# Cross attention in units of four heads by 512 queries, keys resident, softmax sums by matmuls of their own

## Chip, cores and metric

One core of one Trainium2 chip runs the whole program. The metric is device microseconds of one execution; lower is better. The median of three runs of the kernel before is 3451.21 us (3448.59 to 3453.72).

## What is computed

A pre-norm decoder layer in float32: self attention, cross attention with a context of 154 positions, and a gated feed-forward with selected experts. B = 2, S = 2048, D = 512, 16 heads of 32. The change touches cross attention and its two neighbours. In terms of the reference:

```python
q = heads(xq)                     # (2, 16, 2048, 32)
k, v = heads(ctx @ Wk), heads(ctx @ Wv)   # (2, 16, 154, 32)
scores = q @ k.T / sqrt(32)       # padding mask; causal mask key <= query
attn = softmax(scores) @ v        # joined, then Wo, residual, layer norm, feed-forward
```

The causal mask hides something only from the first 154 queries of a batch, so only in the first block of 512. The padding mask is all false in the inputs but is applied.

## The kernel before

The program is a row of stages, each a `nc.Block` that ends with a barrier of all engines: `project_qkv`, `self_attention`, `attention_to_queries`, `cross_context`, `cross_attention`, `shared_feed_forward`, `selected_experts`. They pass tensors on through DRAM.

`cross_context` (L1076) makes keys and values of the context and the masks. It stores the keys as three parts of 32 rows (`xk_parts`: high, high, low), the values with columns of ones between those of each pair of heads (`xv_ones`), and masks for causal and for other blocks.

`cross_attention` (L1194) works in 64 units of two heads by 512 queries. For each unit `load` (L1260) brings the queries' parts, the pair's keys, and its values with ones. The maxima come first: `scores` (L1312) makes queries x keys on TensorE, four tiles of 128 queries for each head, each with a mask matmul behind it (L1327). `maxima` (L1380) takes the negative maximum over 154 keys of four tiles at once on VectorE (L1383) and splits it into three bfloat16 parts with five small operations (L1392 to L1397). `turn_max` (L1330) transposes the parts with eight matmuls, and `max_rows` (L1399) copies them into three more rows of the query tile, so that the transposed scores come out with the maximum taken off. `transposed_scores` (L1338) makes keys x queries, in two halves of 77 keys. ScalarE takes the exponential (L1429), and `weighted_values` (L1349) multiplies with the 64 columns of values and ones of a head: one half of the output's partitions per head, and the sums of the softmax come out beside the weighted values. ScalarE copies both out (L1433), and SP stores values and sums. TensorE's order is written out by hand:

```python
for w in range(UPB):                       # L1367
    pe.wait_ge(max_rows_done, at(i, w, 1, 1))
    transposed_scores(i, b, causal, w, 0)
    turn_max(*after(i, w, 1))
    scores(*after(i, w, 2), (0,))
    transposed_scores(i, b, causal, w, 1)
    scores(*after(i, w, 2), (1,))
    weighted_values(i, w)
```

During the first units GpSimd also splits the next stage's weights into a high and a low part (`Ahead`, L52; `split`, L65), after some memsets at the stage's head (L1299).

`shared_feed_forward` (L1438) works on eight blocks of 512 rows. It first loads all sums, inverts them on VectorE (L1643), stores them, and reads the inverses back for each block with every row repeated 32 times (`load_sums`, L1540). GpSimd multiplies the weighted values with them and adds the output bias to the residual (`scale`, L1599: L1602 once, L1604 four times); then ScalarE (`split`, L1759) and VectorE split the product for TensorE's three-part matmuls. In a block's end, `transposes` (L1813) wait for VectorE's `norm` (L1678, the instruction is L1686), between the matmuls of `down` (L1846) and those of `up` (L1822).

`self_attention` (L324) is not changed, but has already the form that cross attention gets: units of four heads, values in four groups of 32 columns (L583), sums by a matmul with ones (L591, L598), reciprocals in PSUM (L677) and a product (L684).

## Time and profile before

| | us |
|---|---|
| median of three runs | 3451.21 |
| the profiled execution, its own time | 3448.84 |
| its span, first to last instruction | 3446.9 |
| TensorE busy (matmuls) | 3077.2 |
| VectorE busy | 2216.5 |
| ScalarE busy | 1609.8 |
| GpSimd busy | 1745.6 |

The mean granted TensorE clock is 0.943 of full speed. Busy times are over the whole span, so they mix stages with different limits: a stage is to be read in its own stretch. PE is TensorE's matmuls, PEld its weight loads, DVE VectorE, ACT ScalarE, POOL GpSimd, SP the engine that issues DMAs.
### The profile page before, as it was taken

The page shows a single profiled execution, that of the slowest core. Times are in us where ns is not written, and L with a number is a line of the kernel's source. Part 1 is how long each engine was busy: PE and PEld are TensorE (multiplying, and loading weights), DVE is VectorE, ACT ScalarE, POOL GpSimd, SP SyncE. Part 2 cuts the span into 40 slices and gives each one's busy share as a digit, 9 for nine tenths or more (in the row PEclk, how much of TensorE's full clock was granted, in tenths as well). Part 3 has the DMA queues.
Part 4 walks back from the last instruction along what each step waited for, and adds up shares of the span by engine and source line. Part 5 has one row for each costly group of instructions (what it writes and reads, how often), then busy time and mean ns, then how long its engine had stood idle before and what let it go on. Part 6 is the DMA issues. An engine that isn't in the chain of part 4 may idle for free. (4 is left out here: it accounts for less than half of the span.)

```text
span 3446.9 us, 44367 instructions
## 1 busy us (share of the span) xinstructions
PE 3077.2 (89%) x15510; PEld 1769.8 (51%) x15510; DVE 2216.5 (64%) x4046; ACT 1609.8 (47%) x2933; POOL 1745.6 (51%) x701
## 2 busy tenths in 40 slices
PE   7997999999999999999999994896499994888578
PEld 6875444444444544444444441784255553666433
DVE  4334788888888888888888871563366663666322
ACT  2221466666666666666666664231145451222111
POOL 0001378787887878888788886000200002444255
PEclk9998799999999999999999997997699997999679
DMA  4546445646346464464645344696544444432631
GB/s 173 182 170 176 108 100 110 132 92 151 85 107 147 89 150 95 101 141 101 150 86 110 75 92 121 179 243 163 137 123 123 123 123 138 147 146 110 216 86 34
DMA packets 195323, 442.85 MB, mean 128 GB/s; under 512 B 32618, under 2 KB 60202, under 8 KB 175532
## 3 DMA queue, kind: packets, MB, share of 16 engines
q1 hardware_dynamic: 171014, 295.73, 29.3%
q0 software_dynamic: 24128, 144.75, 19.9%
q8 instruction: 109, 1.79, 0.2%
q14 instruction: 72, 0.59, 0.1%
HBM read 187.47 MB, written 126.04 MB: 91 GB/s over the span
## 5 line engine op out<-in xcount | busy, mean ns | idle before, releaser
L652 DVE TENSOR_REDUCE part_max<-ps_s 128x1 f32<-128x512 f32 x2048 | 1270.1, 679 | 309.9 <-PE ps_s L553 309.9
L749 ACT ACTIVATE probs<-ps_st 128x512 f32<-128x512 f32 x2048 | 1086.4, 600 | 546.0 <-PE ps_st L572 531.6
L511 POOL TENSOR_TENSOR added<-added,probs 128x2048 f32<-128x2048 f32 x256 | 1182.5, 4619 | 91.1 <-ACT probs L749 64.7
L553 PE MATMUL ps_s<-k_stack,q_stack 96*128 96x512 f32 x2048 | 841.9, 427 | 28.3 <-POOL max_parts L501 20.6
L572 PE MATMUL ps_st<-q_stack,k_stack 98*128 98x512 f32 x2048 | 857.2, 424 | 6.6 <-ACT probs L749 5.4
L572 PEld LDWEIGHTS ps_st<-q_stack,k_stack 98*128 98x128 f32 x2048 | 386.6, 189 | 504.6 <-ACT probs L749 363.1
L583 PE MATMUL ps_pv<-probs,v_sb 128*32 128x512 f32 x4096 | 546.5, 606 | 0.0
L553 PEld LDWEIGHTS ps_s<-k_stack,q_stack 96*128 96x128 f32 x2048 | 395.5, 193 | 214.5 <-DVE part_max L652 143.7
L519 POOL DMA_DIRECT2D probs<-probs x128 | 112.8, 881 | 230.8 <-PE ps_pv L583 218.2
L1626 POOL MEMSET e_bias_rows<- 128x1024 f32 x1 | 1.0, 953 | 370.0 <-POOLq L46 370.0
L511 POOL TENSOR_TENSOR added<-probs 128x2048 f32<-128x2048 f32 x32 | 146.3, 4571 | 48.7 <-ACT probs L749 48.7
L677 DVE RECIPROCAL ps_d<-ps_d 128x128 f32<-128x128 f32 x128 | 120.9, 949 | 63.2 <-PE ps_d L598 63.2
L1325 PE MATMUL xps_s<-xk_stack,xq_stack 96*128 96x154 f32 x528 | 130.4, 335 | 31.8 <-DMA xv_ones_sb<-xv_ones 31.8
L583 PEld LDWEIGHTS ps_pv<-probs,v_sb 128*32 128x32 f32 x4096 | 80.7, 108 | 152.1 <-ACT probs L749 123.4
L1401 DVE CAST xq_stack<-xps_s 3x1024 fp32r<-3x1024 f32 x65 | 79.9, 1230 | 97.4 <-PE xps_s L1334 97.4
L1325 PEld LDWEIGHTS xps_s<-xk_stack,xq_stack 96*128 96x128 f32 x528 | 108.5, 208 | 60.8 <-issue 33.8
L1355 PE MATMUL xps_pv<-xprobs,xv_ones_sb 128*64 128x512 f32 x512 | 124.8, 607 | 10.1 <-ACT xprobs L1429 9.3
L1429 ACT ACTIVATE xprobs<-xps_st,xpad_bias 77x512 f32<-77x512 f32 x192 | 120.5, 678 | 28.3 <-PE xps_st L1343 28.2
L1383 DVE TENSOR_REDUCE xneg_max<-xps_s 128x4 f32<-128x616 f32 x132 | 105.6, 800 | 34.9 <-PE xps_s L1327 33.0
L227 DVE TENSOR_TENSOR qk_l_out<-ps_g,qk_h_out 128x512 fp32r<-128x512 f32 x64 | 43.3, 689 | 126.1 <-ACT qk_h_out L264 126.1
L185 POOL TENSOR_TENSOR rstd<-var_eps,minus_half 128x4 f32<-128x4 f32 x8 | 8.1, 1015 | 224.5 <-DVE var_eps L205 224.5
L1327 PE MATMUL xps_s<-mq_sb,xident_bf 128*128 128x154 bf16 (+1 forms) x528 | 115.7, 249 | 0.0
(269 smaller groups left out, 3684.6 us busy)
## 6 DMA issues: line engine op xcount, KB each, us to landing
probs<-probs POOLq DMA_DIRECT2D x128, 1024.0 KB, 7.1
xq_stack<-q_parts SPq DMA_DIRECT2D x66, 384.0 KB
q_stack<-q_hi SPq DMA_DIRECT2D x64, 256.0 KB
k_stack<-k_hi SPq DMA_DIRECT2D x64, 256.0 KB, 10.7
q_parts<-q_h_out SPq DMA_DIRECT2D x64, 256.0 KB, 4.9
x_in<-in_x_rows SPq DMA_DIRECT2D x8, 1024.0 KB
q_hi<-qk_h_out SPq DMA_DIRECT2D x8, 1024.0 KB
q_lo<-qk_l_out SPq DMA_DIRECT2D x8, 1024.0 KB, 6.4
```

Of the source, the lines that this page charges most:

```text
L511: pool.tensor_tensor(added[:, w % 2], left, probs[:, k % RING], ALU.add).then_inc(added_up, 1)
L519: pool.dma_start(probs[:, k % RING].rearrange("p j q -> p (j q)"), probs[:, (k - 1) % RING].rearrange("p j q -> p (j q)"), accum_op=ALU.ad ...
L553: pe.matmul(ps_s[:, place % BANKS], q_stack[0:ROWS, w % 4, j, t * P:(t + 1) * P], k_stack[0:ROWS, w // BPB, j, n * BLK:(n + 1) * BLK], sta ...
L572: pe.matmul(ps_st[:, n % BANKS], k_stack[:, w // BPB, j, k * P:(k + 1) * P], q_stack[:, w % 4, j], start=True, stop=True).then_inc(item_do ...
L583: mm = pe.matmul(ps_pv[j * HD:(j + 1) * HD], v_sb[:, w // BPB, k, j * HD:(j + 1) * HD], probs[:, k % RING, j], start=(k == 0), stop=(k == ...
L652: dve.tensor_reduce(part_max[:, s:s + 1], ps_s[:, (w * SLOTS + s) % BANKS], AX.X, ALU.max)\
L677: dve.reciprocal(ps_d[:, cols], ps_d[:, cols]).then_inc(inverted, 1)
L749: act.activation(probs[:, k % RING, j], ps_st[:, n % BANKS], ACT.Exp, scale=SCALE).then_inc(item_used, 1)
L1325: pe.matmul(out, q_stack[0:ROWS, w % BUFS, j, t * P:(t + 1) * P], k_stack[0:ROWS, w % BUFS, j], start=True, stop=False)
L1327: mm = pe.matmul(out, ident_bf[:], mask_of(mq, i)[:, t], start=False, stop=True)
L1355: mm = pe.matmul(ps_pv[j * 2 * HD:(j + 1) * 2 * HD, w % 2], v_ones[:, w % BUFS, h, j * HD:(j + 2) * HD], probs[:, (w % 2) * 2 + j, h], sta ...
L1429: act.activation(probs[0:KH, (w % 2) * 2 + j, h], ps_st[0:KH, h], ACT.Exp, scale=SCALE, **bias)\
```

## The change

Cross attention goes over 32 units of four heads by 512 queries. The keys of a batch are loaded once into two tiles that stay: one for the scores, with a further row for the padding bias, one for the transposed scores. Queries are loaded by unit, the values once. Mask matmuls are left for causal blocks only. The maxima are taken over two query tiles at a time into three PSUM banks, split into two parts instead of three, turned by four matmuls, and copied by ScalarE. `weighted_values` has four groups of 32 columns, and `totals`, behind it, multiplies the exponentials of both key halves with ones. VectorE inverts the sums in PSUM in four pieces and multiplies; the output is stored normalized. The loops are unrolled. GpSimd's split of the weights keeps its operations in another order. The feed-forward loses the sums: their load, inversion, store, broadcast loads and the multiply. `cross_context` stores plain values, masks for causal blocks alone, and two small tensors with the padding bias.

The core of the diff, indentation cut by part; the lines removed from `cross_attention` are those of the kernel printed above.

```diff
-def split(self, pool):
-    pool.wait_ge(self.loaded, 16 * len(self.weights))
-    for _, raw, high, _ in self.weights:
+def split_step(self, pool, step):
+    n = step // 2
+    _, raw, high, low = self.weights[n]
+    if step % 2 == 0:
+        pool.wait_ge(self.loaded, 16 * len(self.weights))
         pool.tensor_copy(high, raw).then_inc(self.high_done, 1)
-    for n, (_, raw, high, low) in enumerate(self.weights):
+    else:
         pool.wait_ge(self.high_done, n + 1)
         pool.tensor_tensor(low, raw, high.bitcast(F32), ALU.subtract).then_inc(self.low_done, 1)
-    pool.wait_ge(self.low_done, len(self.weights))
...
-    sp.wait_ge(ones_set, 1)
-    for b in range(B):
-        sp.dma_start(xv_ones[b], xv[:, b].rearrange("k h r c -> k (h r c)")).then_inc(stored, 16)
-    sp.wait_ge(masks_done, 4 * B)
-    sp.dma_start(mask_q, mq[:].rearrange("p b f t k -> p (b f t k)")).then_inc(stored, 16)
-    sp.dma_start(mask_k, mk[:].rearrange("p b f h k -> p (b f h k)")).then_inc(stored, 16)
-    sp.wait_ge(stored, 16 * (3 * (P // HD) + B + 2))
-@block.gpsimd
-def _(pool):
-    pool.memset(xv[:, :, :, :, HD:2 * HD], 1.0).then_inc(ones_set, 1)
+    sp.dma_start(xv_rows, xv[:]).then_inc(stored, 16)
+    sp.wait_ge(masks_done, 3 * B + 1)
+    sp.dma_start(bias_rows.unsqueeze(0), bias_row[0:1]).then_inc(stored, 16)
+    sp.dma_start(bias_scaled, scaled_col[:]).then_inc(stored, 16)
+    sp.dma_start(mask_q, mq[:].rearrange("p b t k -> p (b t k)")).then_inc(stored, 16)
+    sp.dma_start(mask_k, mk[:].rearrange("p b h k -> p (b h k)")).then_inc(stored, 16)
+    sp.wait_ge(stored, 16 * (3 * (P // HD) + 5))
...
+HEADS = 4
+QUADS = H // HEADS
+UNITS = NBLK * QUADS
...
+TOP = ROWS + 2
+SLOTS = HEADS * TPB // 2
+TILES = HEADS * 2
+BEFORE_TURN = 3
+BANKS = 3
...
+kt_stack = sb("xkt_stack", [TOP, B, H, SC], F32R)
+ks_stack = sb("xks_stack", [TOP + 1, B, H, SC], F32R)
+q_stack = sb("xq_stack", [TOP + 1, BUFS, HEADS, BLK], F32R)
+v_sb = sb("xv_sb", [KH, B, 2, D])
+ones = sb("xones", [KH, HD])
+probs = sb("xprobs", [KH, 2, 2, HEADS, BLK])
+neg_max = sb("xneg_max", [P, 2, HEADS, TPB])
+max_parts = sb("xmax_parts", [P, TPB, P], F32R)
...
+ps_st = ctx.enter_context(nc.psum_tensor("xps_st", [P, BANKS, BLK], F32))
+ps_s = ctx.enter_context(nc.psum_tensor("xps_s", [P, BANKS, BLK], F32))
+ps_pv = ctx.enter_context(nc.psum_tensor("xps_pv", [P, BLK], F32))
+ps_d = ctx.enter_context(nc.psum_tensor("xps_d", [P, BLK], F32))
...
+def exists(u):
+    return 0 <= u < UNITS
+def batch(u):
+    return u // (BPB * QUADS)
+def causal(u):
+    return u // QUADS % BPB == 0
+def item(u, t):
+    return 1 + u * (TILES + 1) + t + (1 if t >= BEFORE_TURN and exists(u + 1) else 0)
+def turn_item(u):
+    return 1 + (u - 1) * (TILES + 1) + BEFORE_TURN if u else 0
+out_units = attn_t.rearrange("b (g p) (n k) -> b n g p k", p=P, k=BLK)
...
+def load_q(u):
+    for h in range(2):
+        sp.dma_start(q_stack[0:ROWS, u % BUFS, 2 * h:2 * h + 2].bitcast(F32),
+                     q_parts[u // QUADS, 2 * (u % QUADS) + h]).then_inc(q_loaded[u % BUFS], 16)
+def load_k(b):
+    sp.dma_start(ks_stack[0:ROWS, b].bitcast(F32), xk_parts[:, b]).then_inc(k_loaded[b], 16)
+    sp.dma_start(ks_stack[TOP:TOP + 1, b].bitcast(F32),
+                 pad_row[b].unsqueeze(0).unsqueeze(0).to_broadcast([1, H, SC])).then_inc(k_loaded[b], 16)
+    sp.dma_start(kt_stack[0:ROWS, b].bitcast(F32), xk_parts[:, b]).then_inc(k_loaded[b], 16)
+sp.wait_ge(ones_set, 2)
+load_q(0)
+load_k(0)
+sp.dma_start(ident[:], eye).then_inc(consts_loaded, 16)
 sp.dma_start(ident_bf[:], eye_bf).then_inc(consts_loaded, 16)
+sp.dma_start(mq[:].rearrange("p b t k -> p (b t k)"), mask_q).then_inc(consts_loaded, 16)
 sp.wait_ge(ones_set, 4)
+sp.dma_start(mk[0:KH].rearrange("p b h k -> p (b h k)"), mask_k).then_inc(consts_loaded, 16)
+sp.dma_start(pad_bias[:], pad_scaled).then_inc(consts_loaded, 16)
+load_q(1)
+sp.dma_start(v_sb[:], xv_rows).then_inc(v_loaded, 16)
+load_q(2)
+load_q(3)
+load_k(1)
 ahead.load(sp)
+for u in range(UNITS + 2):
+    if exists(u - 2):
+        n, g = (u - 2) // QUADS, (u - 2) % QUADS
+        sp.wait_ge(normalized, u - 1)
+        sp.dma_start(out_units[n // BPB, n % BPB, g], attn_out[:, u % 2]).then_inc(out_stored[u % 2], 16)
+    if exists(u + BUFS):
+        sp.wait_ge(item_done, item(u, TILES - 1) + 1)
+        load_q(u + BUFS)
 for s in range(2):
+    sp.wait_ge(out_stored[s], 16 * UNITS // 2)
...
+    for n, (tile, value) in enumerate(((q_stack[ROWS:TOP + 1].bitcast(F32), 1.0), (ks_stack[ROWS:TOP + 1].bitcast(F32), 0.0),
+                                       (kt_stack[ROWS:TOP].bitcast(F32), 1.0), (mk[:], 0.0),
+                                       (max_parts[:].bitcast(F32), 0.0), (ones[:], 1.0))):
+        if n:
+            pool.wait_ge(ones_set, n)
+        pool.memset(tile, value).then_inc(ones_set, 1)
+    pool.wait_ge(ones_set, 6)
+    for step in range(ahead.STEPS):
+        ahead.split_step(pool, step)
+    pool.wait_ge(ahead.low_done, len(weights_ahead))
 @block.tensor
 def _(pe):
+    def scores(u, s):
+        j, half = s // 2, s % 2
+        place = u * SLOTS + s
+        if place >= BANKS:
+            pe.wait_ge(max_done, place - BANKS + 1)
+        if s == 0:
+            pe.wait_ge(q_loaded[u % BUFS], 32 * (u // BUFS + 1))
+            pe.wait_ge(k_loaded[batch(u)], 48)
+        for i in range(2):
+            t = 2 * half + i
+            out = ps_s[:, place % BANKS, i * SC:(i + 1) * SC]
+            top = ROWS if causal(u) else TOP + 1
+            mm = pe.matmul(out, q_stack[0:top, u % BUFS, j, t * P:(t + 1) * P],
+                           ks_stack[0:top, batch(u), u % QUADS * HEADS + j], start=True, stop=not causal(u))
+            if causal(u):
+                mm = pe.matmul(out, ident_bf[:], mq[:, batch(u), t], start=False, stop=True)
+        mm.then_inc(scores_done, 1)
+    def turn_max(u):
+        n = turn_item(u)
+        pe.wait_ge(max_low, u + 1)
+        if n >= BANKS:
+            pe.wait_ge(item_used, n - BANKS + 1)
+        for t in range(TPB):
+            mm = pe.matmul(ps_st[:, n % BANKS, t * P:(t + 1) * P], max_parts[:, t], ident_r[:],
+                           start=True, stop=True)
+        mm.then_inc(item_done, 1)
+    def transposed_scores(u, t):
+        j, h = t // 2, t % 2
+        n = item(u, t)
+        if t == 0:
+            pe.wait_ge(item_used, turn_item(u) + 1)
+        if n >= BANKS:
+            pe.wait_ge(item_used, n - BANKS + 1)
+        out = ps_st[0:KH, n % BANKS]
+        mm = pe.matmul(out, kt_stack[:, batch(u), u % QUADS * HEADS + j, h * KH:(h + 1) * KH],
+                       q_stack[0:TOP, u % BUFS, j], start=True, stop=not causal(u))
+        if causal(u):
+            mm = pe.matmul(out, ident_bf[:, 0:KH], mk[:, batch(u), h], start=False, stop=True)
+        mm.then_inc(item_done, 1)
+    def weighted_values(u):
+        pe.wait_ge(v_loaded, 16)
+        pe.wait_ge(item_used, item(u, TILES - 1) + 1)
+        if u:
+            pe.wait_ge(raw_done, u)
         for h in range(2):
+            for j in range(HEADS):
+                c = (u % QUADS * HEADS + j) * HD
+                mm = pe.matmul(ps_pv[j * HD:(j + 1) * HD], v_sb[:, batch(u), h, c:c + HD], probs[:, u % 2, h, j],
                                start=(h == 0), stop=(h == 1))
         mm.then_inc(pv_done, 1)
+    def totals(u):
+        if u:
+            pe.wait_ge(normalized, u)
+        for h in range(2):
+            for j in range(HEADS):
+                mm = pe.matmul(ps_d[j * HD:(j + 1) * HD], ones[:], probs[:, u % 2, h, j],
+                               start=(h == 0), stop=(h == 1))
+        mm.then_inc(dens_done, 1)
+    pe.wait_ge(ones_set, 6)
+    pe.wait_ge(consts_loaded, 80)
+    pe.wait_ge(ident_ready, 1)
+    for s in range(SLOTS):
+        scores(0, s)
+    for s in range(BEFORE_TURN):
+        scores(1, s)
+    turn_max(0)
+    for s in range(BEFORE_TURN, SLOTS):
+        scores(1, s)
+    for u in range(UNITS + 1):
+        for t in range(TILES):
+            if t == BEFORE_TURN:
+                if exists(u + 1):
+                    turn_max(u + 1)
+                if exists(u - 1):
+                    weighted_values(u - 1)
+                    totals(u - 1)
+            if exists(u):
+                transposed_scores(u, t)
+            if exists(u + 2):
+                scores(u + 2, t)
 @block.vector
 def _(dve):
+    def slot_max(u, s):
+        dve.wait_ge(scores_done, u * SLOTS + s + 1)
+        dve.tensor_reduce(neg_max[:, u % 2, s // 2, s % 2 * 2:s % 2 * 2 + 2],
+                          ps_s[:, (u * SLOTS + s) % BANKS, 0:2 * SC].rearrange("p (t k) -> p t k", k=SC),
+                          AX.X, ALU.max, negate=True).then_inc(max_done, 1)
+    def max_rows(u):
+        parts = max_parts[:].rearrange("p t (j c) -> p j t c", j=HEADS)
+        dve.wait_ge(max_done, (u + 1) * SLOTS)
+        if u:
+            dve.wait_ge(item_done, turn_item(u - 1) + 1)
+        dve.tensor_copy(parts[:, :, :, 0], neg_max[:, u % 2]).then_inc(max_high, 1)
+        dve.wait_ge(max_high, u + 1)
+        dve.tensor_tensor(parts[:, :, :, 1], neg_max[:, u % 2], parts[:, :, :, 0].bitcast(F32), ALU.subtract)\
+           .then_inc(max_low, 1)
+    def invert(u, q):
+        cols = slice(q * P, (q + 1) * P)
+        dve.wait_ge(dens_done, u + 1)
+        dve.reciprocal(ps_d[:, cols], ps_d[:, cols]).then_inc(inverted, 1)
+    def normalize(u):
+        dve.wait_ge(raw_done, u + 1)
+        if u >= 2:
+            dve.wait_ge(out_stored[u % 2], 16 * (u // 2))
+        dve.wait_ge(inverted, TPB * (u + 1))
+        dve.tensor_tensor(attn_out[:, u % 2], ps_d[:], attn_raw[:, u % 2], ALU.mult).then_inc(normalized, 1)
+    def slots(u, first, end):
+        for s in range(first, end):
+            slot_max(u, s)
+    dve.wait_ge(consts_loaded, 80)
+    dve.tensor_copy(ident_r[:], ident[:]).then_inc(ident_ready, 1)
+    dve.wait_ge(ones_set, 6)
+    for u in range(2):
+        slots(u, 0, SLOTS)
+        max_rows(u)
+    for u in range(UNITS + 2):
+        for s in range(SLOTS):
+            if exists(u + 2):
+                slot_max(u + 2, s)
+            if exists(u - 2) and s < 2:
+                invert(u - 2, s + 2)
+            if exists(u - 2) and s == 2:
+                normalize(u - 2)
+            if exists(u - 1) and 3 <= s < 5:
+                invert(u - 1, s - 3)
+        if exists(u + 2):
+            max_rows(u + 2)
 @block.scalar
 def _(act):
+    def max_rows(u):
+        n = turn_item(u)
+        act.wait_ge(item_done, n + 1)
+        for j in range(HEADS):
+            mm = act.activation(q_stack[ROWS:TOP, u % BUFS, j], ps_st[j * HD:j * HD + 2, n % BANKS], ACT.Copy)
+        mm.then_inc(item_used, 1)
+    def exponentials(u, t):
+        if t == 0 and u >= 2:
+            act.wait_ge(dens_done, u - 1)
+        n = item(u, t)
+        bias = {} if causal(u) else {"bias": pad_bias[:, batch(u), t % 2:t % 2 + 1]}
+        act.wait_ge(item_done, n + 1)
+        act.activation(probs[:, u % 2, t % 2, t // 2], ps_st[0:KH, n % BANKS], ACT.Exp, scale=SCALE, **bias)\
+           .then_inc(item_used, 1)
+    def raw_out(u):
+        if u >= 2:
+            act.wait_ge(normalized, u - 1)
+        act.wait_ge(pv_done, u + 1)
+        act.activation(attn_raw[:, u % 2], ps_pv[:], ACT.Copy).then_inc(raw_done, 1)
+    act.wait_ge(ones_set, 6)
+    act.wait_ge(consts_loaded, 80)
+    max_rows(0)
+    for u in range(UNITS + 1):
+        for t in range(TILES):
+            if t == BEFORE_TURN:
+                if exists(u + 1):
+                    max_rows(u + 1)
+                if exists(u - 1):
+                    raw_out(u - 1)
+            if exists(u):
+                exponentials(u, t)
...
-def load_rows(n, u):
+def load(n, u):
     sp.dma_start(a_raw[:, u], a_blocks[n // BPB, n % BPB]).then_inc(loaded[u], 16)
     sp.dma_start(x_in[:, u], x1_blocks[n]).then_inc(loaded[u], 16)
-def load_sums(n, i, u):
-    b, k = n // BPB, n % BPB
-    if not first(i, u):
-        sp.wait_ge(scaled, count(i, u, 1, 0))
-    for c in range(DC):
-        src = inv_blocks[b, k, c].unsqueeze(1).to_broadcast([P // HD, HD, BLK])
-        sp.dma_start(a_inv[:, c], src).then_inc(loaded[u], 16)
-def load(n, i, u):
-    load_rows(n, u)
-    load_sums(n, i, u)
-sp.dma_start(sums_sb[:], sums.rearrange("h (n k) -> (h n) k", k=BLK)).then_inc(sums_loaded, 16)
-load_rows(0, 0)
+load(0, 0)
 for dst, src in ((ident[:], eye), (bias_raw[:, 0:D], b12.unsqueeze(0)), (bias_raw[:, D:2 * D], b3.unsqueeze(0)),
                  (bo_all[:], bo.partition_broadcast(P)), (gamma_all[:], gamma.partition_broadcast(P)),
                  (beta_all[:], beta.partition_broadcast(P))):
     sp.dma_start(dst, src).then_inc(w_loaded, 16)
-sp.wait_ge(inv_made, 1)
-sp.dma_start(inv_sums.rearrange("h (n k) -> (h n) k", k=BLK), inv_sb[:]).then_inc(inv_stored, 16)
-sp.wait_ge(inv_stored, 16)
-load_sums(0, 0, 0)
-load(1, 0, 1)
+load(1, 1)
...
-def scale(i, u):
+def add_bias(i, u):
     pool.wait_ge(loaded[u], i * (16 * LOADS) + 16 * LOADS)
-    pool.tensor_tensor(a_raw[:, u], a_raw[:, u], a_inv[:], ALU.mult).then_inc(scaled, 1)
     for t in range(TPB):
         pool.tensor_tensor(x_in[:, u, t], x_in[:, u, t], bo_all[:], ALU.add).then_inc(bo_added, 1)
...
-dve.wait_ge(sums_loaded, 16)
-dve.reciprocal(inv_sb[:], sums_sb[:]).then_inc(inv_made, 1)
...
-act.wait_ge(scaled, count(i, u, 1, 1))
+act.wait_ge(loaded[u], i * (16 * LOADS) + 16 * LOADS)
```

## Rows read from the trace of the kernel before

**Rows 1.** Windows by stage: start:end, length, busy us (count) by engine, clock, DMA share, GB/s.

```profile
2435.40:2453.00 17.60, 0.00 (x0) 0.00 (x0) 0.17 (x1) 0.00 (x0) 8.77 (x4) 0.50 0.54 143
2453.00:2852.50 399.50, 373.19 (x2408) 212.12 (x2408) 253.95 (x527) 187.92 (x320) 16.01 (x6) 0.96 0.43 120
2852.50:2889.60 37.10, 0.00 (x0) 0.00 (x0) 7.87 (x4) 1.91 (x1) 10.70 (x9) 0.50 0.59 180
```

**Rows 2.** ScalarE's timeline, cross attention, copies ending a unit: start us, us, instruction.

```profile
2471.94 0.60 ACT L1433 ACTIVATE xattn_out<-xps_pv 128x512 f32<-128x512 f32 x1 [2.66 <-PE xps_pv L1355]
...
2491.43 0.60 ACT L1433 ACTIVATE xattn_out<-xps_pv 128x512 f32<-128x512 f32 x1 [3.52 <-PE xps_pv L1355]
...
2848.53 0.60 ACT L1433 ACTIVATE xattn_out<-xps_pv 128x512 f32<-128x512 f32 x1 [2.04 <-PE xps_pv L1355]
```

**Rows 3.** TensorE's timeline, one unit of cross attention outside causal blocks.

```profile
2562.24 0.69 PE L1343 MATMUL xps_st<-xq_stack,xk_stack 99*77 99x512 f32 x2
2562.86 0.61 PE L1334 MATMUL xps_s<-xident_bf,xmax_parts 128*3 128x128 bf16 x8
2563.40 0.34 PE L1325 MATMUL xps_s<-xk_stack,xq_stack 96*128 96x154 f32 x1
...
2564.79 0.34 PE L1325 MATMUL xps_s<-xk_stack,xq_stack 96*128 96x154 f32 x1
...
2566.01 1.94 PE L1355 MATMUL xps_pv<-xprobs,xv_ones_sb 128*64 128x512 f32 x8 [0.20 <-ACT xprobs L1429]
2567.87 0.46 PE L1343 MATMUL xps_st<-xq_stack,xk_stack 99*77 99x512 f32 x1
```

**Rows 4.** TensorE's timeline in self attention: values, then sums, of four heads.

```profile
1209.93 1.06 PE L583 MATMUL ps_pv<-probs,v_sb 128*32 128x512 f32 x8
1210.81 1.04 PE L598 MATMUL ps_d<-added,ones 128*32 128x512 f32 x8
```

**Rows 5.** Groups by line: line, engine, operation, tiles, count | busy us, mean ns | idle.

```profile
L1429 ACT ACTIVATE xprobs<-xps_st,xpad_bias 77x512 f32<-77x512 f32 x192 | 120.5, 678 | 28.3 <-PE xps_st L1343 28.2
...
L1383 DVE TENSOR_REDUCE xneg_max<-xps_s 128x4 f32<-128x616 f32 x132 | 105.6, 800 | 34.9 <-PE xps_s L1327 33.0
```

**Rows 6.** VectorE's timeline in self attention: reciprocal, maximum, product, maxima.

```profile
1217.38 0.95 DVE L677 RECIPROCAL ps_d<-ps_d 128x128 f32<-128x128 f32 x1
1218.24 0.63 DVE L652 TENSOR_REDUCE part_max<-ps_s 128x1 f32<-128x512 f32 x1
1218.78 0.67 DVE L684 TENSOR_TENSOR attn_out<-ps_d,attn_raw 128x512 f32<-128x512 f32 x1
1219.37 1.87 DVE L652 TENSOR_REDUCE part_max<-ps_s 128x1 f32<-128x512 f32 x3
```

**Rows 7.** GpSimd's timeline, head of cross attention.

```profile
2436.13 3.51 POOL L1299 MEMSET xprobs<- 128x4096 f32 x1
```

**Rows 8.** VectorE's timeline in unit 2 of cross attention.

```profile
2471.37 4.50 DVE L1394 TENSOR_TENSOR xrest<-xneg_max,xmax_parts 128x8 f32<-128x8 f32 x1
```

**Rows 9.** Timeline of the feed-forward's head.

```profile
2862.89 0.68 DVE L1646 CAST e_bias_rows<-e_bias_raw 1x1024 fp32r<-1x1024 f32 x1 [4.22 <-DMA e_beta_all<-in_shared_beta]
...
2880.43 4.50 POOL L1602 TENSOR_TENSOR e_a_raw<-e_a_raw,e_a_inv 128x2048 f32<-128x2048 f32 x1 [26.21 <-DMA e_a_inv<-inv_sums]
```

**Rows 10.** VectorE's and TensorE's timelines, ends of two feed-forward blocks.

```profile
2985.13 5.31 DVE L1686 TENSOR_SCALAR h_out<-x,e_moments,e_rstd 128x512 f32<-128x512 f32 x2
...
2991.30 1.98 DVE L1686 TENSOR_SCALAR h_out<-x,e_moments,e_rstd 128x512 f32<-128x512 f32 x2
...
2986.60 0.63 PE L1857 MATMUL e_ps_f<-shared_w_h,e_zt_l 128*128 128x512 f32 x2
...
2996.12 1.09 PE L1833 MATMUL e_ps_f<-xwo_w_h,e_xt_h 128*128 128x512 f32 x4
...
3187.22 0.62 PE L1857 MATMUL e_ps_f<-shared_w_h,e_zt_l 128*128 128x512 f32 x2
...
3191.30 1.08 PE L1833 MATMUL e_ps_f<-xwo_w_h,e_xt_h 128*128 128x512 f32 x4
```

248 lines of the change are left out of this document (43 added, 205 removed).

## The prediction

> **What bounds the kernel now.** The windows view by stage comes first [rows 1]. It cuts out the stages that the diff touches: 17.6 us at the head of cross attention with no matrix work, then 399.5 us of cross attention with TensorE busy 373, then 37.1 us at the head of the shared feed-forward with TensorE idle. Each stage ends in a barrier, so what one saves reaches the end undiminished.
>
> Next the ScalarE timeline, for the copy that ends each unit of two heads [rows 2]: units 2 to 64 take (2848.53 - 2491.43) / 62 = 5.76 us on average, while unit 2 alone came 19.49 us after unit 1. Then TensorE inside one unit without causal mask [rows 3]: from 2562.24 to 2567.87, 5.63 us. Two transposed scores take 0.62, the turn of the maxima (eight small matmuls) 0.54, the next 1.39 hold four scores with masks and two transposed scores, with a wait for VectorE in front of 2564.79; four scores with masks and a wait for ScalarE take 1.22; values and sums 1.86. So TensorE's order sets the pace, with some 0.6 us of waits for VectorE's maxima and ScalarE's exponentials. Four heads cost 11.26 us. Of those 62 units 14 are causal and longer: 48 x 5.63 leaves 6.2 for each of them, 12.4 for four heads. VectorE and ScalarE are busy for 254 and 188 of the 399.5 us [rows 1]: room on average, but what counts is the order of the work in a unit.
>
> **Cross attention, one unit of four heads.** The work on TensorE, in terms of this trace:
> - transposed scores: 8 before and after, 0.23 each (four matmuls of 512 columns last 1.09 to the end of the last [rows 10]): 1.9.
> - scores: 16 before and after; the 16 mask matmuls go outside causal blocks (the pad bias rides in one more row of the contraction). The 1.39 above, less two transposed scores and some wait, leave a score with its mask a slot of 0.20 to 0.23. Without the mask a score costs between half of that and all of it; I take 0.13: 2.1 for 3.3.
> - turn: 4 matmuls of 128 columns in place of 2 x 8; I take 0.4 for 1.08.
> - values: 8 matmuls in four column groups, where there were 8 in two groups (2 x 1.86 = 3.72). Self attention has this very form: 8 instructions (four matmuls) start 0.88 us before the next group [rows 4], so 16 cost 1.76. The sums are the same again with ones as weights, the second of the two groups in [rows 4]: 1.76, and 0.1 at the end.
> Sum: 1.9 + 2.1 + 0.4 + 3.6 = 8.0 for 11.26. The columns of ones gave the sums free; now they cost what the narrower groups save, so values and sums are worth nothing net. The score slot has a page against it. The Trainium skill (TensorE: Matmul & The Clock Gate, Part 2: What happens when you issue a matmul) says that weights load behind a running matmul and that N columns cost N cycles; the pair would be 2 x 154 / 2.4 GHz = 0.13 us, an estimate; with its 0.20 the trace disagrees. By the page the 16 scores would cost 1.0.
>
> ScalarE: 8 exponentials of 0.678 [rows 5], 5.4; four copies of two max rows by 512 columns, which I take at the 0.60 of the output copy's 512 columns [rows 2], 2.4; one copy of the output 0.6: 8.4 at most. VectorE: a maximum over 308 columns in place of 616 (0.800, [rows 5]). Self attention's 512 columns go at 0.62 apart and at 0.54 ahead of a reciprocal [rows 6]; 204 columns fewer at 1.04 ns are 0.21 less, so 0.41 and 0.33. Eight: 2.9. New are four reciprocals of 128x128 in PSUM, 0.86 apart [rows 6], 3.5, and a product, 0.59 apart and 0.67 long [rows 6], 0.6; two small operations 0.45. Sum 7.4.
>
> No engine's sum sets the pace; **a chain does**. In TensorE's order totals(u-1) stands ahead of transposed score 3 and scores(u+2, 3), and it waits for normalize(u-2), since ps_d has one buffer. VectorE's next instruction after normalize(u-2) is the maximum over scores(u+2, 3). So VectorE stands idle from normalize to those scores, and everything it does in a unit lies between two totals. Round it goes: product and semaphore 0.73, totals 1.85, a transposed score 0.23, two scores 0.18, 0.28 until VectorE sees them: 3.27. Then VectorE from slot 3 to the next product: 0.34 + 0.86 + 0.34 + 0.86 + 0.41 + 0.41 + 0.43 + 0.45 (max parts) + 0.34 + 0.86 + 0.34 + 0.86 + 0.36 = 6.9. **Period 10.2 us**. I laid TensorE and ScalarE against it: with totals ended at 0, scores 7 wait for a bank until 2.4, the last scores VectorE needs are out by 4.9, the turn at 4.9, values 5.3 to 7.1, then 1.3 us idle for the product; ScalarE ends its exponentials at 4.2 and the max rows at 7.8. Both fit. Causal units: a mask behind each transposed score and score adds 0.2 to 0.4 to the chain, and TensorE's own sum reaches 10.7; I take 10.6. Thirty rounds: 22 x 10.2 + 8 x 10.6 = 309.
>
> **Ends of the stage.** GpSimd's memsets come first: 8192 elements a partition for the max rows at the 3.51 us per 4096 of [rows 7] are 7.0, 4.2 for each key tile's rows, then the mask. SP issues nothing before the second ends, at 11.4, and TensorE needs queries, the keys of a batch twice and constants, 3.1 MB. At the 143 GB/s of the old head that is 22 us, at the 180 of the feed-forward's head 17 [rows 1]; I take the latter, whose transfers are as large: first score at 28 (26 to 34), for 17.6. From there: scores of two units at half clock (granted 0.50 in [rows 1], the lower of the two levels) and max rows 12.6; rounds 0 and 1, 9.5 and 11; thirty rounds 309; the end 12 (values, totals, four reciprocals and a product with nothing under them, store) where 4 to 6 stood. Together 354. Two stalls: the 19.49 us of unit 2 hold 13.3 lost, because tiny VectorE operations took 4.50 while GpSimd split the next stage's weights [rows 8]. The split is moved, not removed; VectorE has now two such operations for four heads where it had ten, and I keep 7 (0 to 13). The loads are queued as 7.5 MB ahead of unit 4's queries: 2 (0 to 8). Stage: 28 + 354 + 7 + 2 = 391 for 417.1, **-26**. The context stage stores half the masks and the values once: two issues of some 1.8 us become shorter, three small ones are added: -1.5 (-3 to +1). Key and value loads gone from SP's steady state and 2 big query loads per four heads kept are at nothing: the chain hides them, two units ahead.
>
> **Feed-forward.** Its head: sums are loaded, inverted, stored, and read back 32-fold by four DMAs; GpSimd's multiply waited for them until 2880.43 and took 4.50, though the constants, queued behind the first rows, were in at 2862.89 [rows 9]. Now ScalarE splits straight from the rows: 2884.93 - 2862.89 = **-22**. It needs the first two loads, which stood ahead of those constants; the loads for block 1 now follow at once and are not due for 15 us.
> In each later block: GpSimd's multiply of 4.6 us is gone. While it ran, VectorE's two norm operations took 5.31 us; beside the four shorter adds two take 1.98 [rows 10]. From the last matmuls of down 2 to the first full group of up it is 2986.60 to 2996.12, 9.52; in the last pair, where GpSimd has neither multiply nor adds, 3187.22 to 3191.30, 4.08 [rows 10]. So 5.44 is the upper bound; the adds stay, and now start where the multiply did, under both pairs of norms: 2 x 0.9 of it stays. Saved 3.5 a block (1.9 to 5.4), six blocks with the pattern: **-21**. With 1 for an earlier rsqrt: **-44** (-34 to -56).
>
> **Sum.** -26 - 1.5 - 44 = -71.5. The profiled execution had 3448.84 around its span of 3446.9; the median of the runs is 3451.21. 3451.2 - 71.5 = 3379.7; I say 3380.
>
> **Rivals.** *Cross attention gains nothing*: another 0.8 us a round from latencies that I set too low (a reciprocal and a PSUM maximum in turn, the semaphores) gives the 26 back: 3406. For: the chain has some twenty hand-overs. Against: every duration in it stands in self attention's rows. Chance 0.17. *More gain*: the chain 0.5 shorter, the block at its bound of 5.4: -15 -12, 3353. Chance 0.15.
> *Slower*: TensorE's clock. The old stage ran at 0.96 with hardly a gap [rows 1]; the new one leaves TensorE idle 2.2 us of 10.2, in a gap of 1.3 ahead of totals and small ones between. At half clock throughout, TensorE's 8.0 become 15.7, and that is the period: 30 x 5.5 = 165 more, 3545. It turns the sign at 12.6 a round (72 / 30 = 2.4 more). Half clock on the totals alone (1.85 more) gives 3435. The Trainium skill warns of this (TensorE: Matmul & The Clock Gate, HAM oscillation — how this bites in real kernels: gaps in TensorE's work throttle its clock again and again). Against: most of each round is busy, and in the feed-forward, where TensorE loses 5.4 us a block to waits, the next group of four still takes 1.09, as the 1.08 of the block without them [rows 10]. Slower 0.05, the milder form 0.06. The change not doing what it says, the four column groups running one by one with 77 rows where self attention has 128, would add about 10 us a round; nothing in the trace hints at it: 0.02, in the slower chance.
>
> **Numbers.** Forecast 0.55. The range takes in 3406 and 3353 and the bounds of the heads, 3345 to 3412; outside stay the clock cases. 0.2% (7 us) is what a measurement can tell from no change. Faster 0.92, same 0.01, slower 0.07.
>
> **What would show it.** VectorE waiting some 2.5 us once a round for scores with TensorE's totals under it, TensorE waiting for the product ahead of totals, ScalarE's output copies 10.2 apart, first score 28 us into the stage, feed-forward's first matmul 22 us earlier in its stage, blocks 36.5 apart instead of 40. Wrong if the period is ScalarE's or TensorE's, if the clock falls under 0.9 in the stage, or if the blocks stay at 40.

## The result, and the profile after

| | us |
|---|---|
| kernel before, 11 runs | 3449.83 (3445.78 to 3454.89) |
| kernel after, 11 runs | 3420.66 (3396.12 to 3439.86) |
| ratio | 0.9903 [0.9874, 0.9933] |
| profiled execution of after, span | 3418.9 |

The change makes the kernel 29 us faster, a little under 1%. 72 were forecast, and 3420.66 lies outside the range of 3345 to 3412. The runs of after spread over 44 us where those of before spread over 9. A ratio is made of undisturbed runs alone (the highest run of e1_cover and of e5_low below is left out of it), and it is not the quotient of the two medians, so it differs a little from that.

Every run of an experiment is compared with runs of the kernel before on the same chip. The kernel after was timed in other rounds than the experiments, and the three groups of experiments ran on three chips. Where kernels of different groups are set side by side, or an experiment beside the kernel after, it goes by each one's distance from the kernel before, whose medians lie between 3442.9 and 3449.8.

The windows by stage, of the kernel after (columns as in [rows 1]; I cut cross attention at its first score, at 2588.8, 2690 and 2820):

```profile
2432.80:2462.80 30.00, 0.00 (x0) 0.00 (x0) 0.23 (x1) 0.00 (x0) 17.78 (x6) 0.50 0.61 149
2462.80:2588.80 126.00, 113.02 (x729) 67.90 (x729) 83.17 (x168) 83.18 (x141) 16.16 (x6) 0.88 0.47 131
2588.80:2690.00 101.20, 101.18 (x438) 54.69 (x438) 48.34 (x95) 52.45 (x82) 0.00 (x0) 0.50 0.23 65
2690.00:2820.00 130.00, 114.70 (x820) 62.07 (x819) 93.14 (x190) 98.95 (x167) 0.00 (x0) 1.00 0.35 100
2820.00:2862.30 42.30, 32.42 (x130) 9.71 (x128) 18.64 (x27) 16.53 (x28) 0.02 (x1) 0.55 0.07 26
2862.30:2879.30 17.00, 0.00 (x0) 0.03 (x1) 6.09 (x3) 1.91 (x1) 7.70 (x8) 0.50 0.77 282
```

The third line is the one to see: for 101 us TensorE's granted clock is 0.50, the lower of its two levels (1.2 GHz in place of 2.4), while TensorE is busy all the time. In the stage before, the clock was 0.96 over the whole [rows 1]. The stage now takes 429.5 us, from 2432.8 to 2862.3, where it took 417.1 and I forecast 391; the head of the feed-forward (last line) fell from 37.1 to 17.0.

The copies that end a unit on ScalarE (as [rows 2]; now one for four heads):

```profile
2490.89 0.60 ACT L1476 ACTIVATE xattn_raw<-xps_pv 128x512 f32<-128x512 f32 x1
2504.69 0.60 ACT L1476 ACTIVATE xattn_raw<-xps_pv 128x512 f32<-128x512 f32 x1 [1.22 <-PE xps_pv L1364]
...
2578.63 0.60 ACT L1476 ACTIVATE xattn_raw<-xps_pv 128x512 f32<-128x512 f32 x1
2588.67 0.60 ACT L1476 ACTIVATE xattn_raw<-xps_pv 128x512 f32<-128x512 f32 x1
2603.34 0.60 ACT L1476 ACTIVATE xattn_raw<-xps_pv 128x512 f32<-128x512 f32 x1 [1.28 <-PE xps_pv L1364]
2617.51 0.60 ACT L1476 ACTIVATE xattn_raw<-xps_pv 128x512 f32<-128x512 f32 x1 [1.28 <-PE xps_pv L1364]
...
2697.25 0.60 ACT L1476 ACTIVATE xattn_raw<-xps_pv 128x512 f32<-128x512 f32 x1
...
2807.46 0.60 ACT L1476 ACTIVATE xattn_raw<-xps_pv 128x512 f32<-128x512 f32 x1
2817.48 0.60 ACT L1476 ACTIVATE xattn_raw<-xps_pv 128x512 f32<-128x512 f32 x1
...
2851.27 0.60 ACT L1476 ACTIVATE xattn_raw<-xps_pv 128x512 f32<-128x512 f32 x1 [3.86 <-PE xps_pv L1364]
```

At full clock they are 10.03 us apart (2578.63 to 2588.67, 2807.46 to 2817.48). At half clock they are 14.17 apart (2603.34 to 2617.51). From 2588.67 to 2697.25 seven rounds take 108.6.

One round at full clock, TensorE's and VectorE's timelines of the kernel after (cf. [rows 3]):

```profile
2545.95 1.92 PE L1364 MATMUL xps_pv<-xprobs,xv_sb 77*32 77x512 f32 x16
2548.72 1.92 PE L1373 MATMUL xps_d<-xprobs,xones 77*32 77x512 f32 x16 [0.85 <-DVE xattn_out L1429]
...
2550.87 0.35 PE L1325 MATMUL xps_s<-xks_stack,xq_stack 99*128 99x154 f32 x2
...
2588.82 3.64 PE L1373 MATMUL xps_d<-xprobs,xones 77*32 77x512 f32 x16 [0.85 <-DVE xattn_out L1429]
```

```profile
2547.99 0.67 DVE L1429 TENSOR_TENSOR xattn_out<-xps_d,xattn_raw 128x512 f32<-128x512 f32 x1
2551.25 0.48 DVE L1404 TENSOR_REDUCE xneg_max<-xps_s 128x2 f32<-128x308 f32 x1 [2.59 <-PE xps_s L1325]
```

This is the chain as forecast: TensorE waits 0.85 for the product, totals take 1.9, VectorE waits 2.59 for the scores behind them. In the last line of the first block, after such a wait, totals take 3.64: here the clock falls. Also to be seen: values and totals run over 77 rows by 32 columns. In the kernel before the values ran over 128 by 64 [rows 3]; its tile of exponentials had zeros in the rows above 77.

The feed-forward: GpSimd's rsqrt of a block, then VectorE's and TensorE's rows at a block's end (cf. [rows 10]):

```profile
2931.67 1.02 POOL L1645 TENSOR_TENSOR e_rstd<-e_var_eps,e_minus_half 128x4 f32<-128x4 f32 x1 [5.36 <-DVE e_var_eps L1702]
...
3152.75 1.02 POOL L1645 TENSOR_TENSOR e_rstd<-e_var_eps,e_minus_half 128x4 f32<-128x4 f32 x1 [5.37 <-DVE e_var_eps L1702]
```

```profile
2970.36 2.04 DVE L1712 TENSOR_SCALAR h_out<-x,e_moments,e_rstd 128x512 f32<-128x512 f32 x2
...
2971.83 0.63 PE L1883 MATMUL e_ps_f<-shared_w_h,e_zt_l 128*128 128x512 f32 x2
...
2977.89 1.09 PE L1859 MATMUL e_ps_f<-xwo_w_h,e_xt_h 128*128 128x512 f32 x4
```

Blocks come (3152.75 - 2931.67) / 6 = 36.85 us apart. In the kernel before it was (3183.82 - 2943.24) / 6 = 40.10:

```profile
2943.24 1.02 POOL L1617 TENSOR_TENSOR e_rstd<-e_var_eps,e_minus_half 128x4 f32<-128x4 f32 x1 [5.36 <-DVE e_var_eps L1676]
...
3183.82 1.02 POOL L1617 TENSOR_TENSOR e_rstd<-e_var_eps,e_minus_half 128x4 f32<-128x4 f32 x1 [5.37 <-DVE e_var_eps L1676]
```

Two norms take 2.04 where they took 5.31, and the gap from down to up is 6.06 for 9.52.

### The profile page after: what moved, and what is told of

The parts are those of the page before. It is cut to its first block and busy times, and to the rows that moved or that the text cites. A ratio compares the mean times of both kernels' runs of the same rounds, so it can differ in the third digit from the quotient of the medians.

```text
span 3418.9 us, 41782 instructions
## 1 busy us (share of the span) xinstructions
PE 3061.5 (90%) x15214; PEld 1750.2 (51%) x15214; DVE 2181.1 (64%) x3987; ACT 1672.3 (49%) x3029; POOL 1718.2 (50%) x694
## 5 line engine op out<-in xcount | busy, mean ns | idle before, releaser
L555 PE MATMUL ps_s<-k_stack,q_stack 96*128 96x512 f32 x2048 | 842.1, 427 | 28.3 <-POOL max_parts L503 20.6
L1404 DVE TENSOR_REDUCE xneg_max<-xps_s 128x2 f32<-128x308 f32 x256 | 110.6, 448 | 130.8 <-PE xps_s L1325 82.2
L1325 PE MATMUL xps_s<-xks_stack,xq_stack 99*128 99x154 f32 (+1 forms) x512 | 130.7, 336 | 49.1 <-DVE xident_r L1436 38.7
L1325 PEld LDWEIGHTS xps_s<-xks_stack,xq_stack 99*128 99x128 f32 (+1 forms) x512 | 116.4, 234 | 76.8 <-issue 43.4
L1422 DVE RECIPROCAL xps_d<-xps_d 128x128 f32<-128x128 f32 x128 | 120.5, 948 | 19.4 <-PE xps_d L1373 19.4
L1350 PE MATMUL xps_st<-xq_stack,xkt_stack 98*77 98x512 f32 x256 | 122.9, 487 | 1.0 <-ACT xq_stack L1460 0.8
L1460 ACT ACTIVATE xq_stack<-xps_st 2x512 fp32r<-2x512 f32 x128 | 75.2, 588 | 70.7 <-PE xps_st L1338 69.1
```

The source lines that it names most:

```text
L555: pe.matmul(ps_s[:, place % BANKS], q_stack[0:ROWS, w % 4, j, t * P:(t + 1) * P], k_stack[0:ROWS, w // BPB, j, n * BLK:(n + 1) * BLK], sta ...
L1325: mm = pe.matmul(out, q_stack[0:top, u % BUFS, j, t * P:(t + 1) * P], ks_stack[0:top, batch(u), u % QUADS * HEADS + j], start=True, stop=n ...
L1350: mm = pe.matmul(out, kt_stack[:, batch(u), u % QUADS * HEADS + j, h * KH:(h + 1) * KH], q_stack[0:TOP, u % BUFS, j], start=True, stop=not ...
L1422: dve.reciprocal(ps_d[:, cols], ps_d[:, cols]).then_inc(inverted, 1)
```

## The experiments

What had to be explained was the fallen clock. **Theory A**: it is the gap ahead of totals, 0.85 us a round. **Theory B**: the new work asks too much of the chip. **Theory C**: chance, whatever the kernel. Later two more: **D**, what TensorE is busy with counts, not that it is busy; and **E**, idle time and the kind of work count together. Twelve kernels in three groups (e1 to e4, e5 to e8, e9 to e12), each timed in several rounds beside the kernel before. The mean clock is that of the profiled execution, over the whole span:

| kernel | median (lowest to highest) | before | ratio | mean clock |
|---|---|---|---|---|
| e1_cover | 3388.8 (3374.7 to 3435.3) | 3444.1 | 0.9825 [0.9809, 0.9840] | 0.940 |
| e2_late | 3468.7 (3458.8 to 3473.5) | 3444.1 | 1.0068 [1.0055, 1.0082] | 0.901 |
| e3_gap | 3482.4 (3478.7 to 3484.6) | 3444.1 | 1.0107 [1.0092, 1.0121] | 0.895 |
| e4_ff | 3404.0 (3403.1 to 3409.5) | 3444.1 | 0.9886 [0.9872, 0.9900] | 0.947 |
| e5_low | 3436.4 (3422.4 to 3500.8) | 3445.1 | 0.9985 [0.9963, 1.0008] | 0.920 |
| e6_wide | 3380.7 (3373.0 to 3404.1) | 3445.1 | 0.9825 [0.9800, 0.9850] | 0.943 |
| e7_rows | 3364.7 (3361.4 to 3366.1) | 3445.1 | 0.9767 [0.9754, 0.9780] | 0.945 |
| e8_late4 | 3351.3 (3347.5 to 3353.5) | 3445.1 | 0.9726 [0.9713, 0.9738] | 0.939 |
| e9_masks | 3377.5 (3373.3 to 3380.5) | 3442.9 | 0.9802 [0.9787, 0.9817] | 0.947 |
| e10_late_rows | 3331.6 (3326.5 to 3338.1) | 3442.9 | 0.9678 [0.9660, 0.9696] | 0.948 |
| e11_head | 3327.0 (3319.8 to 3330.0) | 3442.9 | 0.9654 [0.9638, 0.9669] | 0.946 |
| e12_rows_gap | 3395.3 (3391.9 to 3397.6) | 3442.9 | 0.9857 [0.9839, 0.9875] | 0.943 |

### The feed-forward by itself: e4_ff

```diff
 cross_attention(nc, q_parts, xk_parts, xv_ones, mask_q, mask_k, ...)     # of before
-shared_feed_forward(nc, x1_rows, attn2_t, sums2, inv_sums2, w_h, ...)
+shared_feed_forward(nc, x1_rows, attn2_t, w_h, ...)                      # of after
```

> The cross attention of the kernel before (units of two heads) with the feed-forward of the kernel after; the division by the sums of the softmax is left out of the computation. Forecast of the feed-forward alone: 44 us less than the kernel before, 3406, with the small scatter of the kernel before. Read from the trace of the changed kernel: its head 20 less, six blocks 3.3 less each: 3409. If the feed-forward gained less because the clock also falls there after the new cross attention, this one comes out under 3400.

Measured: 40.1 us less than before, a third more than the whole change brings. So the new cross attention with its context stage, as it is, *costs* about 11 us; in the two traces its stage takes 429.5 - 417.1 = 12.4 more. The forecast for the feed-forward was 44; a head 20 shorter where I said 22, and six blocks each 40.10 - 36.85 = 3.2 shorter where I said 3.5, make up the 40.

### The gap ahead of totals: e1_cover, e3_gap

e1_cover, with its helper function written out in place:

```diff
 weighted_values(u - 1)
+if exists(u):
+    pe.wait_ge(item_used, n - BANKS + 1)             # n = item(u, 3)
+    for _ in range(4):
+        pe.matmul(ps_st[0:KH, n % BANKS], ident_bf[:, 0:KH], mk[:, 0, 0], start=True, stop=True)
 totals(u - 1)
```

> Four matmuls that nobody reads (bfloat16, 77 x 512) go between the weighted values and the wait ahead of totals, so that TensorE works through the 0.85 us in which it waited for the product; VectorE's chain stays as it is. Theory A (that gap lets TensorE's clock fall, and the fallen clock is all that the changed kernel lacks of the forecast): granted clock 0.99 through the rounds, output copies 10.0 to 10.1 apart everywhere, about 3380 us, and runs within 15 us of each other instead of 44. Theory B (the clock falls because the new stage asks too much of the chip, more matmul instructions in four column groups a round, not too little): more work makes it no better, 3420 or more and the same scatter. Theory C (the clock goes with neither, only with the chance of the execution): like the changed kernel, 3395 to 3440.

e3_gap:

```diff
 dve.wait_ge(inverted, TPB * (u + 1))
+dve.reciprocal(more_inv[:], ps_d[:, 0:P]).then_inc(more_done, 1)
+dve.wait_ge(more_done, u + 1)
 dve.tensor_tensor(attn_out[:, u % 2], ps_d[:], attn_raw[:, u % 2], ALU.mult).then_inc(normalized, 1)
```

> One more reciprocal of 128 x 128, whose result nobody reads, ahead of each product: the chain is 0.86 us longer, TensorE's gap ahead of totals 1.7 in place of 0.85. At an unchanged clock this costs 32 x 0.86 = 27 us: 3448. Theory A: the larger gap lets the clock fall more often or for longer, so more than that: 3470 to 3530, mean granted clock under 0.91. Theory B: TensorE works less per us, so the clock falls less: under 3440. Theory C: 3448 with the same scatter.

More work in the gap made the kernel 55 us faster than before, against B. A larger gap made it 38 us slower than before: from -29 to +38 is 67, of which the longer chain is 32 x 0.86 = 27. That is against C. Both go the way of A. But e1_cover does not hold the clock throughout, as A had it: its mean clock is 0.940, one of its six runs is at 3435, and the windows of its profiled execution show the clock down for a while:

```profile
2520.00:2565.00 45.00, 42.37 (x294) 21.08 (x293) 32.30 (x65) 34.30 (x58) 0.00 (x0) 1.00 0.37 110
2565.00:2612.00 47.00, 44.37 (x240) 20.70 (x236) 28.15 (x58) 29.25 (x49) 0.00 (x0) 0.78 0.29 85
2612.00:2700.00 88.00, 86.08 (x624) 46.08 (x620) 60.38 (x123) 63.79 (x107) 0.00 (x0) 1.00 0.33 96
```

The window of e3_gap between the two sets of causal rounds: TensorE is busy without a break, at half clock. The gap that was put in is gone there, since at half clock TensorE's own work fills the round, and still the clock stays down.

```profile
2530.00:2690.00 160.00, 160.00 (x690) 87.46 (x686) 91.94 (x176) 92.56 (x143) 0.00 (x0) 0.50 0.25 74
```

### Order alone: e2_late, e8_late4

e2_late, and in the last comment e8_late4:

```diff
 weighted_values(u - 1)
-totals(u - 1)                                # at t == 3
+                                             # totals(u - 1) at t == 5
...
-if exists(u - 1) and 3 <= s < 5:
-    invert(u - 1, s - 3)
+if exists(u - 1) and 5 <= s < 7:             # e8_late4: 4 <= s < 6, s - 4
+    invert(u - 1, s - 5)
```

> Totals and the first two reciprocals go two steps later in the order of a round (totals ahead of transposed score 5, reciprocals after slot maxima 5 and 6); no work is added or removed. TensorE has two transposed scores and two score slots to do while VectorE makes the product, and VectorE two slot maxima while totals run. Theory A: the chain becomes product 0.73, totals 1.85, semaphore 0.15 and VectorE's 6.4, about 9.1 us a round for 10.03, TensorE busy 8.7 of it, so that the clock stays at 0.98 or more: 3380 less 30 x 0.9 = about 3352, small scatter. Theory B: rounds of 9.1 while the clock is up, and it still falls for some 100 us or more: 3385 to 3415, scatter as before. If the chain was read wrongly, the rounds stay at 10.0.

This was the worst miss: 25 us slower than before. Its timeline of VectorE in a round shows that I had laid out the order badly: slot maximum 5 stands ahead of the first reciprocal, and its scores stand behind totals.

```profile
2513.80 0.48 DVE L1406 TENSOR_REDUCE xneg_max<-xps_s 128x2 f32<-128x308 f32 x1 [2.17 <-PE xps_s L1326]
2514.20 0.96 DVE L1424 RECIPROCAL xps_d<-xps_d 128x128 f32<-128x128 f32 x1
```

So the rounds stayed at 9.98, and the clock did not stay up. That is against A too: the gap ahead of totals is gone in e2_late, and TensorE's longest wait in the rounds ahead of the fall is half a microsecond.

```profile
2526.07 0.45 PE L1326 MATMUL xps_s<-xks_stack,xq_stack 99*128 99x154 f32 x2 [0.51 <-DVE xneg_max L1406]
```

Windows of e2_late, causal and other rounds in turn:

```profile
2500.00:2527.00 27.00, 25.85 (x177) 14.39 (x175) 20.18 (x42) 20.47 (x36) 5.10 (x3) 1.00 0.38 111
2530.00:2690.00 160.00, 160.00 (x674) 84.39 (x672) 80.02 (x160) 88.25 (x137) 0.00 (x0) 0.50 0.23 70
2700.00:2727.00 27.00, 27.00 (x198) 15.22 (x195) 21.10 (x43) 20.31 (x36) 0.00 (x0) 1.00 0.39 109
2750.00:2880.00 130.00, 129.42 (x534) 66.08 (x530) 66.09 (x130) 74.89 (x117) 0.00 (x0) 0.50 0.20 61
```

The clock falls soon after the causal rounds end, stays down for 160 us of unbroken work, and comes back in the next causal rounds, about 2691, as it does in the kernel after. Those rounds have the mask matmuls. That led to theory D: something other than being busy holds the clock. It was not just any mask matmul: those behind the scores alone ran for 33 to 34 us (from 2639.36 in the kernel after, 2654.55 in e2_late, 2664.76 in e3_gap) and did not bring the clock back. It came back only when the transposed scores had theirs too, 19, 3 and 3 us after the first of these (2672.57, 2688.49, 2697.97).

The eighth experiment mends the order:

> Totals ahead of transposed score 5 as in the second experiment, but the first reciprocal right behind slot maximum 4 instead of 5, so that VectorE no longer waits for scores that stand behind totals. At full clock the chain is product 0.73, totals 1.9, semaphore 0.15, VectorE's 6.4: rounds of 9.2 in place of 9.98. Theory A: TensorE busy 8.7 of 9.2, the clock stays: 3350 to 3365. Theory D: the narrow matmuls have a larger share of the time than ever, the clock falls right behind the causal rounds and stays down until the next causal ones: rounds of 14.0 to 14.5, 3445 to 3475.

```profile
2555.72 0.68 DVE L1431 TENSOR_TENSOR xattn_out<-xps_d,xattn_raw 128x512 f32<-128x512 f32 x1
2556.32 0.86 DVE L1406 TENSOR_REDUCE xneg_max<-xps_s 128x2 f32<-128x308 f32 x2
2558.53 0.97 DVE L1424 RECIPROCAL xps_d<-xps_d 128x128 f32<-128x128 f32 x1 [1.36 <-PE xps_d L1374]
...
2564.52 0.67 DVE L1431 TENSOR_TENSOR xattn_out<-xps_d,xattn_raw 128x512 f32<-128x512 f32 x1
```

```profile
2500.00:2520.00 20.00, 19.11 (x89) 9.19 (x89) 12.11 (x22) 9.43 (x16) 8.66 (x4) 0.60 0.17 54
2520.00:2760.00 240.00, 232.29 (x1697) 129.48 (x1693) 195.47 (x395) 202.43 (x346) 0.00 (x0) 1.00 0.38 113
2760.00:2790.00 30.00, 28.05 (x108) 7.42 (x111) 12.26 (x18) 14.36 (x25) 0.00 (x0) 0.53 0.07 26
```

VectorE waits 1.36 where it waited 2.59, a round is 8.8 us (product to product, 2555.72 to 2564.52), the clock is full for 240 us, though not at the stage's two ends, and the kernel is 94 us faster than before. D as I had put it, which expected 3445 or more here, is refuted: the same narrow matmuls, packed closer, hold the clock.

### What TensorE is busy with: e5_low, e6_wide, e7_rows

e5_low and e6_wide, against e1_cover:

```diff
-for _ in range(4):                                     # e1_cover
-    pe.matmul(ps_st[0:KH, n % BANKS], ident_bf[:, 0:KH], mk[:, 0, 0], start=True, stop=True)
+for j in range(HEADS):                                 # e5_low
+    pe.matmul(ps_st[j * HD:(j + 1) * HD, n % BANKS], ones[:], probs[:, (u - 1) % 2, 0, j], start=True, stop=True)
...
+for _ in range(4):                                     # e6_wide
+    pe.matmul(ps_st[:, n % BANKS], ident_bf[:], mk[:, 0, 0], start=True, stop=True)
```

> As the first experiment, with the filler in another form: one more set of four float32 matmuls of 77 rows by 32 columns (the form of totals, 0.92 us, results read by nobody) in place of the four bfloat16 ones of 77 columns (0.85 us), at the same place. Theory A (the gap): as good as those, 3375 to 3400, clock 0.94. Theory D (what keeps the clock up is not that TensorE is busy but what it is busy with: the narrow float32 matmuls of values and totals count little, the masks' bfloat16 matmuls, which the change removed outside causal blocks, count much): the filler does not help, clock 0.92 or less, 3420 or more.

> As the first experiment, with weights of 128 columns in place of 77 in the four filler matmuls: same duration, more of the array at work. Theory A: no difference from it, 3375 to 3400 with now and then a slower run. Theory D: fewer falls of the clock than with 77 columns (which lost 3 x 3 us a fall, four falls): 3365 to 3380, clock 0.945 or more.

e7_rows, against the kernel after:

```diff
-v_sb = sb("xv_sb", [KH, B, 2, D])
-ones = sb("xones", [KH, HD])
-probs = sb("xprobs", [KH, 2, 2, HEADS, BLK])
+v_sb = sb("xv_sb", [P, B, 2, D])                       # rows 77 to 127 set to zero once
+ones = sb("xones", [P, HD])
+probs = sb("xprobs", [P, 2, 2, HEADS, BLK])
```

> No filler; the weighted values and totals run over 128 rows in place of 77, the further rows holding zeros on both sides (some memsets on VectorE in the head, where it has nothing else). Number, duration and order of the instructions stay. Theory A: as the changed kernel, 3396 to 3440. Theory D, if zero rows count like others: clock back at 0.94, 3375 to 3390. If only what moves through the rows counts, zero rows give nothing, and it comes out like the changed kernel.

Windows with the clock, of e5_low (two stretches) and then of e7_rows:

```profile
2520.00:2689.00 169.00, 161.66 (x1217) 86.34 (x1219) 122.28 (x250) 128.20 (x216) 0.00 (x0) 1.00 0.36 105
2700.00:2850.00 150.00, 149.93 (x641) 73.61 (x633) 66.68 (x135) 76.91 (x121) 0.00 (x0) 0.50 0.18 55
```

```profile
2520.00:2640.00 120.00, 104.41 (x761) 56.64 (x757) 88.38 (x180) 92.92 (x156) 0.00 (x0) 1.00 0.35 104
2640.00:2700.00 60.00, 56.07 (x411) 31.06 (x403) 43.50 (x89) 45.28 (x77) 0.00 (x0) 1.00 0.37 106
2700.00:2800.00 100.00, 86.67 (x563) 41.92 (x563) 67.09 (x130) 72.24 (x122) 0.00 (x0) 0.93 0.25 77
```

e5_low fills the same gap with about the same time and does not help: eleven of its twelve runs lie between 3422 and 3466. So A alone falls too: TensorE was busy 96% of the 169 us in which the clock held here, and then lost it for 150. e7_rows has the gap (TensorE busy 87% in its first window) and the same instructions in number and duration; only the rows of values and totals go back to 128, with zeros in them. It holds the full clock for 180 us and never falls for long after that (0.93 over 2700 to 2800), all five runs lie within 5 us, and it is 80 us faster than before. The rows were widened for values and totals at once, on the side of the weights and on that of the exponentials, so which of them counts is not told apart. e6_wide, 64 us faster, is a little better than e1_cover by its median (8 us) with ranges that overlap; the ratios are the same, so whether the further weight columns help is open.

### Undoing the masks, and rows against a gap: e9_masks, e12_rows_gap

```diff
-if causal(u):
-    mm = pe.matmul(out, ident_bf[:], mq[:, batch(u), t], start=False, stop=True)
+mask = mq[:, batch(u), t] if causal(u) else no_mask[:, 0:SC]
+mm = pe.matmul(out, ident_bf[:], mask, start=False, stop=True)
...                                                    # the same behind transposed scores
```

> One part of the change undone: every score and transposed score has a mask matmul behind it again (outside causal blocks with zeros, from a tile set once), 16 of 154 columns and 8 of 512 more a round. Causal rounds at full clock take 10.8 to 11.5 us in the traces, so 22 rounds become some 1.2 longer: 26 us more than the changed kernel at full clock (3380): 3406. Theory E (the clock falls when the array as a whole has too little work in a given time, by idle time, by few rows or by few columns; the removal of the masks took it to the edge): clock at full through all rounds, 3400 to 3412, and runs within 15 us of each other. If the masks' removal has no part in it, the clock still falls: 3440 or more.

> The 128 rows of the seventh experiment with the extra reciprocal of the third: TensorE idles 0.86 us a round more than in the seventh. Theory E, if the rows give enough reserve: 3365 + 27 = 3392, clock 0.94; without the rows the same gap cost 118 us against the seventh. If idle time decides and rows do not: 3470 to 3485 as in the third.

Windows of e9_masks, then of e12_rows_gap:

```profile
2520.00:2640.00 120.00, 120.00 (x956) 70.08 (x954) 85.03 (x171) 95.41 (x149) 0.00 (x0) 1.00 0.33 103
```

```profile
2520.00:2800.00 280.00, 231.60 (x1616) 123.50 (x1614) 210.77 (x405) 196.80 (x330) 0.00 (x0) 0.98 0.32 95
```

With the masks back TensorE is busy throughout, a round is 10.63 us (ScalarE's copies at 2524.29 and 2534.92) and the clock is full: 65 us faster than before. That is 28 better than I expected. About half of it is that the masks lengthen a round by 0.6 us where causal rounds had made me say 1.2, over 22 rounds; the other half is my base of 3380 for full clock, which e7_rows puts at 3365. The removal of these matmuls was to be a gain; by itself, in this kernel, it costs 65 - 29 = 36 us. e12_rows_gap came within 3 us of E's 3392: with 128 rows the gap that took e3_gap to 3482 costs 3395.3 - 3364.7 = 31 us, little more than its own length of 27. TensorE is busy 83% of the time there and the clock is 0.98; the kernel after lost it with 58.76 of 68 us busy, 86%.

```profile
2520.00:2588.00 68.00, 58.76 (x413) 32.05 (x409) 50.78 (x104) 53.12 (x89) 0.00 (x0) 1.00 0.36 105
```

(kernel after, the stretch ahead of the fall). What is shown is that idle time (e3_gap against the kernel after), the rows in use (e7_rows against the kernel after, e12_rows_gap against e3_gap) and the kind of matmul that fills a gap (e5_low against e1_cover) all move it. What the chip counts, these runs don't say. Nor do they say why e2_late, with the same work in 9.98 us as the kernel after in 10.03 and with shorter waits, has a mean clock of 0.898 to 0.905 in all its runs and loses it sooner in its trace; that stays open.

### A version that beats both: e10_late_rows, e11_head

e10_late_rows is e8_late4 and e7_rows together; e11_head adds

```diff
-sp.wait_ge(ones_set, 2)
 load_q(0)
-load_k(0)
 sp.dma_start(ident[:], eye).then_inc(consts_loaded, 16)
...
+load_k(0)                                    # in it: keys, then wait_ge(ones_set, 2), then the pad bias row
 sp.wait_ge(ones_set, 4)
```

> The order of the eighth experiment together with the 128 rows of the seventh. Rounds at full clock stay at 8.79 (eighth experiment). There the clock was at half in 2500 to 2520 and from 2760 on, 12 to 15 us lost; the zero rows kept it up at both places in the seventh. Theory E: about 3338, within 8 us of each other. If the two work through the same reserve, no gain over the eighth: 3350.

> As the tenth, and the loads at the head of cross attention are issued before GpSimd's memsets are done (only the pad bias row and the key mask wait for theirs): the first load goes out 11.4 us earlier. TensorE waits for the key loads, the memsets (19 us) and the constants, so the first score comes at 20 to 24 us into the stage in place of 29: 5 to 9 us less than the tenth, about 3331. If the loads only share the rate of 200 GB/s with those for later units, or the transfers wait elsewhere, nothing.

```profile
2431.51 0.79 SPq L1264 DMA_DIRECT2D xq_stack<-q_parts  x2
```

```profile
2453.16 0.47 PE L1330 MATMUL xps_s<-xks_stack,xq_stack 96*128 96x154 f32 x1 [30.16 <-DVE xident_r L1446]
```

e10_late_rows is 111 us faster than before, e11_head 116 (ratio 0.9654 [0.9638, 0.9669]). In the head of e11_head (the two lines above, SP's queue and TensorE) the first load goes out as GpSimd's memsets start, and the first score comes 21.65 us after that; in e10_late_rows it comes 28.3 after the memsets' start (2430.45 to 2458.75). Of those 6.7 us the medians show 4.6, with ranges that overlap, so that part is seen in the trace rather than in the time.

## Why the prediction was wrong

**The step that failed** is the clock. The sum took every TensorE duration at full clock and so put the clock's cost at nothing. The reason stands in the rivals: "Against: most of each round is busy". Busy time was taken as what holds the clock. The runs showed the clock at half for 101 us in which TensorE was busy for 101.18 of 101.20. The prediction's own sign of being wrong, a clock under 0.9 in the stage, came: from the first score to the end of the stage it is 0.79. e7_rows is that sum very nearly come true: the same instructions and the same chain at almost full clock, 3445.1 - 3364.7 = 80 us gained. The kernel after gained 29. So the lost clock takes some 50 us out of the -71.5 forecast; the other terms together were 9 too cautious.

That the result lies within 15 us of the 3435 of "the milder form" is luck. That form had half clock on totals alone, 1.85 us in every round. What came was whole rounds at half clock, a quarter of the stage in one piece and more at its two ends, and full clock between.

- **TensorE's clock**: forecast at full; half for 101 us and at the stage's two ends. Seven rounds at 108.6 us against 72.1 for the same seven in e7_rows (copies at 2578.60 and 2650.68) are 36.5; the last three, copies 28 to 31, lose 6.8 the same way. Copies 0 to 3 lose 5.9, but part of that is TensorE waiting for VectorE beside GpSimd's split, 1.90 us against 0.83. The whole stage is 429.5 against 377.4 (2431.45 to 2808.88), 52.1 longer; 2.8 of that is a first score that comes later (30.0 against 27.2) for its loads and not for the clock. A round at half clock took 14.17 us, where the rival reckoned with 15.7. I noticed 77 rows for 128, but only as a doubt about column groups.
- **The page**: I cited the Trainium skill (TensorE: Matmul & The Clock Gate, HAM oscillation) as a warning, and the warning was right in kind. It puts the loss down to gaps in TensorE's work. The trace agrees that gaps matter (e3_gap, 38 us slower than before, where the kernel after is 29 faster), and it shows that gaps are not the whole of it: 101 us at 0.50 with TensorE busy for 101.18.
- **The chain**: right. 10.03 us for 10.2; TensorE's wait 0.85 for 1.3, VectorE's 2.59 for 2.5. e8_late4 confirms it from the other side: taking maxima and scores out from under totals shortened a round by 1.2 us.
- **Thirty rounds**: 309 forecast; 346.6 after (2504.69 to 2851.27), 301.4 in e7_rows (copies at 2497.85 and 2799.20).
- **First score**: 28 forecast, 30.0 measured, and bound by the memsets and loads as said.
- **TensorE's own sum**: 8.0 forecast, 8.67 of 10.03 measured (58.76 of 68 us busy); the chain sets the pace, so nothing hung on it. The sum has a score at 0.13 and the chain has two at 0.18, which does not fit together; two took 0.19 (2551.28 to 2551.47 in the kernel after).
- **GpSimd's split**: I kept 7. Two small operations of VectorE took 1.36 and 1.80 us beside it, against 0.18 and 0.19 elsewhere: 2.8. TensorE waited 1.90 us for them, and the clock's first fall stands right behind that wait (0.51 from 2500 to 2510). In e7_rows the wait is 0.83 and the clock stays full; in e12_rows_gap it is 4.80, and the clock is 0.70 over 2500 to 2510 in spite of its 128 rows. No run takes the split away, so that it brought this fall on is likely and not shown.

```profile
2496.75 1.36 DVE L1414 CAST xmax_parts<-xneg_max 128x16 fp32r<-128x16 f32 x1
2498.15 1.80 DVE L1416 TENSOR_TENSOR xmax_parts<-xneg_max,xmax_parts 128x16 fp32r<-128x16 f32 x1
```

- **Feed-forward**: -44 forecast, -40.1 by e4_ff; the mechanism and both terms right, each a little high. The 0.9 a pair that I left to the adds came from no row; the gap from down to up fell by 9.52 - 6.06 = 3.46, as said.
- **Mask matmuls**: costed as pure loss of TensorE time, in a stage whose pace a chain through VectorE sets. With them a round is 10.63, without them 10.03: the 2.0 us they take on TensorE (10.63 busy of 10.63, against 58.76 / 68 x 10.03 = 8.67) are worth 0.6 a round, and with them the clock was held.

## What to carry to other kernels

When an edit takes work off TensorE, or runs its matmuls over fewer rows, read the granted clock in windows of tens of us, not the stage's mean: the saved work can be paid back at half clock, in a stretch in which the engine looks fully busy. Where a chain through another engine leaves TensorE idle each round, first move work out from under the wait (here 1.2 us a round for nothing). And rows that the data leaves empty can be kept, filled with zeros, at no time of their own (totals take 1.92 us over 77 rows and over 128): about 50 us gained here.

## What the runs showed of the hardware

- The lower clock lasted on when TensorE had no gap left. Once down, it stayed so through 101 us (after), 160 us (e2_late, e3_gap) and 150 us (e5_low) of unbroken matmuls. In the first three it came back in rounds with bfloat16 mask matmuls of 128 rows, and only when the transposed scores had theirs too (about 2691 in after and e2_late, 2701 in e3_gap). In e1_cover and e12_rows_gap, which have such matmuls or 128 rows in values and totals in every round, falls were short: no 10 us between 2510 and 2820 are under 0.66 in the one, or under 0.83 in the other.
- With rows of zeros the clock held: e7_rows against the kernel after, full from 2520 to 2700.
- The scatter of the times can be a sign of it. Kernels that lose the clock for a varying time spread over 44 us (after) and 43 (e5_low without its highest run); those that hold it, over 5 (e7_rows) to 12 (e10_late_rows). A small scatter alone says nothing: e3_gap, at half clock for most of the stage, spreads over 6.
